# Grouped-query layer: transposes and a small product moved in front of two score tiles, behind the weighing

## The chip, the cores and the metric

One core of a Trainium2 chip runs the whole kernel as one program. The metric is the device time of one execution in microseconds (us); shown are the median and the spread of three runs. Engines are named as in the profile: PE is TensorE (its weight loads are PEld), DVE is VectorE, ACT is ScalarE, POOL is GpSimd, SP is SyncE.

## The reference

Four transformer-like layers run in a row over x of 8 batches x 512 tokens x 256 features in float32. Each layer normalises x and adds an attention-like part and a feed-forward part to it. The change is in the second layer (called layer 1 in the code), cut here to what matters:

```python
# attention: 16 query heads of width 16, 4 key/value heads, rotary positions
scores = einsum('bhqd,bhkd->bhqk', q, k) / sqrt(256)
p = softmax(scores, axis=-1)
o = einsum('bhqk,bhkd->bhqd', p, v);  attn = o.reshape(B, S, 256) @ Wo
# feed-forward: 64 slots, a gated update of them, and a read by the routing weights alpha
h = gelu(x @ w1x.T + b1);  alpha = softmax over the top 8 of (h @ w2.T + b2) / (|tau| + 0.1)
gi = (alpha.T @ x) / (sum of alpha over tokens)
S_new = GRU(gi, slots)                      # r, z = sigmoid, n = tanh
out = (alpha @ (S_new @ wv.T + bv)) @ wo.T + bo
```

## The kernel before

Layer 1 works batch by batch. Its loop is software-pipelined: one round of MAIN1 holds the back part of one batch (weighing the values, slot update, output) and the front part of the next (projections, scores for the row maxima). PRE1 is the front of the first batch alone, POST1 the back of the last alone, and MAIN1 is run 7 times between them. Each engine has its own instruction stream, written out by hand in program order (`pe1`, `dve1`, `act1`, `sp1`), and the streams meet only at semaphores.

The 16 heads are handled in 4 groups g of 4 heads. For each group the kernel makes two things from queries and keys:

- **Score tiles** `("S", g, i)`, i = 0 to 15, 128 queries x 512 keys. PE makes them in pairs (`two_scores`, L1455), and DVE takes the row maximum of each (`dve_max`, L910). After the 16th, `dve_split_max` (L916, L918) splits the maxima, PE transposes them (tile `("M", g)`, `pe_max_rows`, L543), ACT copies them to `mrow`, and SP sends them through DRAM into an extra row of the query tile.
- **Transposed scores** `("E", g, kt, hp)`, kt = 0 to 3 blocks of 128 keys, hp = 0, 1 pairs of heads (`pe_scores_t`, L557). ACT takes the exponential into `probs` (L816), and `pe_weigh` (L573) multiplies it with the values into `bank_u`.

When a group's four weighings are done, ACT copies `bank_u` to `uraw` (L803), PE transposes that with four transposes into tile `("DT", g)` (`pe_turn_sums`, L756), and DVE normalises it: `dve_normalise_heads` (reciprocal L924, multiply L926, then it waits for its own result and frees the tile). The slot update ends in `h_new` (DVE `blend_slots`, three operations, the last L1766); PE multiplies it with `wvs` into tile `"SV"` (4 products, 8 matmul records in the trace, L1565) and ACT moves it to `svT` (L1649).

**The ring.** The tiles S, M, DT, SV, L, GX, AT, SI and Z2 share three PSUM banks in strict rotation (`Ring` named `sc`: `bank0`, `bank1`, `bank_m`). The rotation follows the order in which `sc_plan1` lists the tiles. The tile at place n can be written only when the reader of the tile at place n-3 has freed it (`vacated`). The reader is DVE for S and DT, ACT for M and SV. `two_scores` waits for both banks of a pair before it issues either.

**Order on PE, groups 2 and 3.** While group 2 is weighed, the score tiles of the next batch's group 0 are made, and while group 3 is weighed those of group 1. For one kt the order is: E of hp 0, two scores (`maxima(0)`), E of hp 1, weighing of the block before (`pe_weigh`), two scores (`maxima(1)`). So a pair of scores stands behind each weighing, and the next pair follows with only one E between. The extra pieces stand behind the second pair:

- g = 2, kt = 1: scores 6 and 7, then DT of group 1.
- g = 2, kt = 3: scores 14 and 15, then (behind the kt loop) SV.
- g = 3, kt = 1: scores 6 and 7, then M of group 0, then DT of group 2.

DVE's stream has the same order: maxima 2 to 5 of group 0, `blend_slots`, maxima 6 and 7, normalise group 1, maxima 8 to 15 and their split, maxima 0 to 7 of group 1, normalise group 2, maxima 8 to 15.

Of the kernel before, what the change touches and what calls it, by code (L numbers as in the profile page):

```python
# [14 lines left out]
P = 128  # L15
BATCH, SEQ, DIM = 8, 512, 256
TT = SEQ // P
KT = DIM // P
# [33 lines left out]
def plans(plan0, plan1, plan2, plan3):  # L52

    return [plan0(FRONT[s], BACK[s]) for s in (PRE0, MAIN0, POST0)] + [plan1(FRONT[s], BACK[s]) for s in (PRE1, MAIN1, POST1)] + plan2 \
        + [plan3(FRONT[s], BACK[s]) for s in (PRE3, MAIN3, POST3)]
# [79 lines left out]
def s_uses(g):  # L135
    return [(("S", g, i), "dve") for i in range(GH * TT)]


def turn_uses(g):
    return [(("DT", g), "dve")]  # L140
# [5 lines left out]
def m_use(g):  # L146
    return [(("M", g), "act")]
# [15 lines left out]
def parts_of(front, back, *items):  # L163

    return [u for part, uses in items if (front if part == "front" else back) for u in uses]
# [24 lines left out]
def sc_plan1(front, back):  # L190
    return parts_of(front, back, ("back", [("AT", "act"), ("SI", "dve")] + s_uses(2)[8:10] + m_use(1) + s_uses(2)[10:]),
                    ("back", s_uses(3)[:8] + m_use(2) + s_uses(3)[8:12]), ("front", [("L", "dve")]),
                    ("back", turn_uses(0) + s_uses(3)[12:] + [("GX", "dve")]),
                    ("front", s_uses(0)[:2]), ("back", m_use(3)), ("front", s_uses(0)[2:8]), ("back", turn_uses(1)),
                    ("front", s_uses(0)[8:]), ("back", [("SV", "act")]),
                    ("front", s_uses(1)[:8] + m_use(0)), ("back", turn_uses(2)), ("front", s_uses(1)[8:]),
                    ("back", [("Z2", "act")]), ("front", s_uses(2)[:2]), ("back", turn_uses(3)), ("front", s_uses(2)[2:8]))


# [63 lines left out]
def build(nc, d, out):  # L263
    ctx = ExitStack()
    with ctx:
# [63 lines left out]
        sc = Ring(sem, "sc", banks + [bank_m], plans(sc_plan0, sc_plan1, NOTHING, sc_plan3))  # L329
# [207 lines left out]
        def pe_max_rows(pe, l, it, g):  # L537

            pe.wait_ge(*maxima_ready(l, it, g))
            for s in sc.vacated(l, it, ("M", g)):  # L540
                pe.wait_ge(*s)
            for qt in range(TT):
                ins = nc.tensor.transpose(sc.tile(l, ("M", g))[0:8, qt * P:(qt + 1) * P],  # L543
                                          msplit[:, g % 2, qt, :, :].rearrange("p a h -> p (a h)"), ident[:])
            ins.then_inc(sc.full.sem, 1)
# [203 lines left out]
        def pe_turn_sums(pe, l, it, g):  # L749

            for s in sc.vacated(l, it, ("DT", g)):
                pe.wait_ge(*s)
            fence(pe)
            pe.wait_ge(*done(pu, l, it, ("U", g)))
            for t in range(TT):
                ins = nc.tensor.transpose(sc.tile(l, ("DT", g))[:, t * P:(t + 1) * P], uraw[:, g % 2, t * P:(t + 1) * P],  # L756
                                          ident[:])
            ins.then_inc(sc.full.sem, 1)
# [514 lines left out]
        wvs = sb("wvs", [P, KT, DIM], F32, l1)  # L1273
# [39 lines left out]
        h_new = sb("h_new", [P, KT, 64], F32, l1)  # L1313
# [24 lines left out]
        h_done = sig("h_done", [0, 1, 0, 0], "vector")  # L1338
# [91 lines left out]
        def pe1(pe, l, it):  # L1430
            front, back = FRONT[l], BACK[l]
# [55 lines left out]
            if back:  # L1487
# [6 lines left out]
                for t in range(TT):  # L1494
                    ins = nc.tensor.transpose(sc.tile(l, "AT")[0:64, t * P:(t + 1) * P], alpha[:, t, :], ident[:])
# [3 lines left out]
                for f in range(KT + 1):  # L1499
                    for t in range(TT):  # L1500
                        lhs = xn[:, t, f * P:(f + 1) * P] if f < KT else ones_sq[:]
                        ins = nc.tensor.matmul(sc.tile(l, "SI")[:, f * 64:(f + 1) * 64], lhs, alpha[:, t, :],
                                               start=(t == 0), stop=(t == TT - 1))
                ins.then_inc(sc.full.sem, 1)
            for g in range(GROUPS):
                for kt in range(TT):
                    cut = SHARE1[2 * kt:2 * kt + 3] if g == 1 else [4 * kt, 4 * kt + 2, 4 * kt + 4]
                    if g == 0:
                        cut = [8 + 2 * kt, 10 + 2 * kt, 10 + 2 * kt]
                    if g == 1 and kt == 0 and not front:  # L1510
                        cut = [0] + cut[1:]

                    def maxima(j):
                        if back if g < 2 else front:
                            scores_of((g + 2) % GROUPS, cut[j], cut[j + 1])

                    if back:
                        pe_scores_t(pe, l, it, g, kt, pair, lambda: maxima(0))
                        if kt == 0 and g < GROUPS - 1:
                            pe_max_rows(pe, l, it, g + 1)  # L1520
                    else:
                        maxima(0)
                    if back and (g or kt):
                        pe_weigh(pe, l, it, GROUPS * g + kt - 1, kv_of_group)
                    if front and g == 0 and kt == 1:
                        pe_transpose_xn(pe, l, it)
                    maxima(1)
                    if front and g == 3 and kt == 1:
                        pe_max_rows(pe, l, it, 0)
                    if front and g == 1 and kt == 1:  # L1530
                        for s in sc.vacated(l, it, "L"):
                            pe.wait_ge(*s)
                        pe.wait_ge(*done(st, l, it, "H"))
                        for t in range(TT):
                            ins = nc.tensor.matmul(sc.tile(l, "L")[:, t * 64:(t + 1) * 64], hid1[:, t * P:(t + 1) * P], w21[:],
                                                   start=True, stop=True)
                        ins.then_inc(sc.full.sem, 1)
                    if back and g and kt == 1:
                        pe_turn_sums(pe, l, it, g - 1)
                if front and g == 0:  # L1540
                    pe.wait_ge(*done(st, l, it, "T"))
                    project("QQ", 0, wq1[:, :, 0:P])
                    last_maxima(0, 2)
                    project("QQ", 1, wq1[:, :, P:2 * P])
                    last_maxima(2, 4)
                    project("KK", 0, wk1[:, :, 0, :], 64)
                    project("KK", 1, wk1[:, :, 1, :], 64)
                    project("H", 0, w1x, P, 1)
                    last_maxima(4, 6)
                if back and g == 1:  # L1550
                    for s in sc.vacated(l, it, "GX"):
                        pe.wait_ge(*s)
                    pe.wait_ge(*gi_done.at(l, it, 1))
                    for j in range(6):
                        for k_ in range(KT):
                            ins = nc.tensor.matmul(sc.tile(l, "GX")[:, j * 64:(j + 1) * 64], wih[:, k_, j * P:(j + 1) * P],
                                                   gi[:, k_, :], start=(k_ == 0), stop=(k_ == 1))
                    ins.then_inc(sc.full.sem, 1)
                if back and g == 2:
                    for s in sc.vacated(l, it, "SV"):  # L1560
                        pe.wait_ge(*s)
                    pe.wait_ge(*h_done.at(l, it, 1))
                    for m in range(KT):
                        for k_ in range(KT):
                            ins = nc.tensor.matmul(sc.tile(l, "SV")[:, m * 64:(m + 1) * 64], wvs[:, k_, m * P:(m + 1) * P],  # L1565
                                                   h_new[:, k_, :], start=(k_ == 0), stop=(k_ == 1))
                    ins.then_inc(sc.full.sem, 1)
            if back:
                for s in sc.vacated(l, it, "Z2"):
# [2 lines left out]
                for k_ in range(KT):  # L1572
                    ins = nc.tensor.matmul(sc.tile(l, "Z2")[0:64, 0:DIM], svT[:, k_, :], wos[:, k_, :],
                                           start=(k_ == 0), stop=(k_ == 1))
# [8 lines left out]
            if back:  # L1583
# [3 lines left out]
                for t in range(TT):  # L1587
                    nc.tensor.matmul(st.tile(l, "OUT")[:, t * DIM:(t + 1) * DIM], alphaT[:, t * P:(t + 1) * P], sv2[:],
                                     start=(t % 2 == 0), stop=False)
# [69 lines left out]
        def dve1(dve, l, it, step):  # L1659
            front, back = FRONT[l], BACK[l]  # L1660
# [107 lines left out]
            def maxima(g, first, last):  # L1768
                for i in range(first, last):
                    dve_max(dve, l, it, step, g, i)  # L1770
                if last == 16:
                    dve_split_max(dve, l, it, step, g, ("S", g, 15))
# [45 lines left out]
            if back:  # L1818
                blend_slots()
            for g in range(2):  # L1820
                for first, last in ((0 if g else 6, 8), (8, 16)):
                    if front:
                        maxima(g, first, last)
                    if back and last == 8:
                        dve_normalise_heads(dve, l, it, step, g + 1)
            if front:
                maxima(2, 0, 2)
# [1677 lines left out]
```

## Time and profile before

| | us |
|---|---|
| median of 3 runs | 3073.55 |
| lowest, highest | 3070.24, 3075.05 |
| profiled execution, its own time | 3092.09 |
| profiled execution, span from first to last instruction | 3090.4 |

| engine | busy us | share of the span |
|---|---|---|
| PE | 2780.4 | 90% |
| DVE | 1868.2 | 60% |
| ACT | 1387.8 | 45% |
| POOL | 394.5 | 13% |

Busy times are sums over the whole span, in which four layers with different limits follow each other. A busy share therefore tells little of one stage: the stage is read from the order of instructions in it, and from what ended each wait. The profiled execution lies 18.5 us above the median of the timed runs; a difference worked out from it is added to the median. Clock is the granted clock of TensorE as a share of full speed (1.00 is 2.4 GHz).

### The profile page before, as it was taken

What the parts mean: (1) busy time and instruction counts of PE and PEld (TensorE: products, weight loads), DVE (VectorE), ACT (ScalarE), POOL (GpSimd) and SP (SyncE); (2) the same over time, 40 slices, a digit from 0 to 9 for tenths busy, and PEclk for the clock granted to TensorE, in tenths of its full rate; (3) what the DMA queues carried; (4) which work ended last, traced back from release to release, by engine and by line L of the source; (5) the groups of instructions that cost most, each with busy time, mean ns of one, the idle gap of its engine ahead of it and who ended that gap; (6) DMA issues with size and microseconds to landing.
All of it is one profiled execution on the core that took longest, in us unless ns stands there. A gap on an engine that the chain in (4) does not pass through costs nothing.

```text
span 3090.4 us, 53706 instructions
## 1 busy us (share of the span) xinstructions
PE 2780.4 (90%) x15686; PEld 1805.8 (58%) x15687; DVE 1868.2 (60%) x4512; ACT 1387.8 (45%) x2011; POOL 394.5 (13%) x373
## 2 busy tenths in 40 slices
PE   4999999999988888888879999999899579999998
PEld 2566556546644444443437777776666356666666
DVE  5666666666637777777737677772122456566653
ACT  1644554454433555555545455432233144444443
POOL 1011001100100000000021211221111312222220
PEclk7999999999987999999999999999999789999999
DMA  6534543654412122221214111122311233333330
GB/s 193 166 119 139 171 140 104 180 152 138 119 39 88 56 70 70 70 69 56 70 51 166 46 36 54 48 89 71 109 62 60 89 98 105 103 102 102 101 98 16
DMA packets 157951, 294.55 MB, mean 95 GB/s; under 512 B 24928, under 2 KB 82657, under 8 KB 149057
## 3 DMA queue, kind: packets, MB, share of 16 engines
q1 hardware_dynamic: 145264, 259.59, 27.8%
q0 software_dynamic: 10464, 28.59, 3.0%
q10 hardware_dynamic: 2160, 5.61, 0.5%
q8 instruction: 31, 0.51, 0.1%
q14 instruction: 32, 0.25, 0.0%
HBM read 194.02 MB, written 99.68 MB: 95 GB/s over the span
## 4 chain that ended last, share of the span: by engine, by line
PE 69%; DVE 12%; DMA 6%; issue 6%; ACT 4%; SPq 2%; DVEq 0%; another core or an unknown queue 0%; POOL 0%; ACTq 0%; POOLq 0%
PE bank_u L573 6%; PE pair L557 5%; PE pair L616 4%; PE bank L1984 4%; PE pair L733 4%; PE pair L2134 4%; DVE nmax L910 3%; PE pair L3074 3%; PE pair L777 3%; PE bank_m L3038 3%; PE bank L534 3%; PE bank L3038 3%; PE bank L2589 3%; PE pair L1482 2%; DMA k_a<-parts_dram 2%
## 5 line engine op out<-in xcount | busy, mean ns | idle before, releaser
L816 ACT ACTIVATE probs<-pair 128x1024 f32<-128x1024 f32 x512 | 502.1, 1021 | 218.7 <-PE pair L557 217.9
L910 DVE TENSOR_REDUCE nmax<-bank 128x1 f32<-128x512 f32 x664 | 441.8, 685 | 175.1 <-PE bank L534 127.0
L910 DVE TENSOR_REDUCE nmax<-bank_m 128x1 f32<-128x512 f32 x360 | 246.5, 685 | 106.7 <-PE bank_m L534 59.8
L573 PE MATMUL bank_u<-probs,vext 128*32 128x512 f32 x2048 | 288.7, 637 | 0.6 <-ACT uraw L803 0.5
L557 PE MATMUL pair<-q_a,k_a 98*128 98x512 f32 x512 | 176.4, 450 | 22.2 <-ACT probs L816 11.8
L534 PE MATMUL bank<-k_a,q_a 96*128 96x512 f32 x336 | 149.3, 479 | 27.4 <-DMA k_a<-parts_dram 24.0
L2282 DVE CUSTOM_DVE_ANT_0 bank<-bank,mask_q 128x128 f32<-128x128 f32 (+1 forms) x320 | 118.8, 420 | 89.5 <-PE bank_m L2024 67.1
L557 PEld LDWEIGHTS pair<-q_a,k_a 98*128 98x128 f32 x512 | 90.3, 202 | 122.0 <-ACT probs L816 66.4
L797 ACT ACTIVATE mrow<-bank 8x512 f32<-8x512 f32 x87 | 50.2, 577 | 231.1 <-PE bank L543 231.1
L2134 PE MATMUL pair<-fc,hid 128*128 128x256 f32 x512 | 133.2, 399 | 6.3 <-ACT probs L2175 6.3
L1455 PE MATMUL bank<-k,q 62*128 62x512 f32 x302 | 113.2, 478 | 26.7 <-DVE nmax L910 26.7
L3110 DVE TENSOR_TENSOR mid<-bank,gate 128x352 f32<-128x352 f32 x73 | 38.3, 524 | 162.1 <-PE bank L3038 162.0
L733 PE MATMUL pair<-w2e,hid 128*128 128x256 f32 x512 | 131.0, 381 | 3.3 <-ACT probs L816 3.3
L557 PE MATMUL pair<-q,k 64*128 64x512 f32 x512 | 116.7, 454 | 15.8 <-DMA q<-m_dram 7.8
L2175 ACT ACTIVATE probs<-pair 128x1024 f32<-128x1024 f32 (+1 forms) x128 | 112.2, 917 | 36.0 <-PE pair L2053 34.5
L474 POOL TENSOR_SCALAR veps<-mv 128x4 f32<-128x4 f32 x31 | 7.3, 235 | 843.9 <-DVE mv L468 839.6
L2967 POOL DMA_INDIRECT xg<-xn,posi x64 | 62.8, 982 | 401.4 <-DVE posi L2815 316.4
L733 PEld LDWEIGHTS pair<-w2e,hid 128*128 128x128 f32 x512 | 94.7, 190 | 30.5 <-issue 15.6
L2134 PEld LDWEIGHTS pair<-fc,hid 128*128 128x128 f32 x512 | 93.1, 194 | 25.5 <-ACT probs L2175 8.2
L534 PEld LDWEIGHTS bank<-k_a,q_a 96*128 96x128 f32 x336 | 65.6, 197 | 72.2 <-DVE nmax L910 26.5
L3074 PE MATMUL pair<-moe_c,midT 128*128 (+1 forms) x432 | 107.2, 384 | 0.0
L803 ACT ACTIVATE uraw<-bank_u 128x512 f32<-128x512 f32 x96 | 57.1, 594 | 110.7 <-PE bank_u L2065 58.9
(471 smaller groups left out, 6036.9 us busy)
## 6 DMA issues: line engine op xcount, KB each, us to landing
parts_dram<-parts SPq DMA_DIRECT2D x64, 512.0 KB
q<-parts_dram SPq DMA_DIRECT2D x126, 128.0 KB
q_a<-parts_dram SPq DMA_DIRECT2D x31, 512.0 KB
k_a<-parts_dram SPq DMA_DIRECT2D x31, 512.0 KB
xs<-xres SPq DMA_DIRECT2D x24, 512.0 KB, 3.1
xl<-xs SPq DMA_DIRECT2D x24, 512.0 KB, 3.9
x_in<-xg SPq DMA_DIRECT2D x74, 128.0 KB, 2.1
yg_dram<-y_out POOLq DMA_DIRECT2D x72, 128.0 KB, 2.0
```

The lines of the kernel that those rows point to most:

```text
L534: nc.tensor.matmul(sc.tile(l, name)[:], q(g, h)[:, qt * P:(qt + 1) * P].bitcast(F32R), k(g, h).bitcast(F32R), start=True, stop=True).then_ ...
L557: ins = nc.tensor.matmul(st.tile(l, name)[:, hh * SEQ:(hh + 1) * SEQ], k[:, kt * P:(kt + 1) * P].bitcast(F32R), q.bitcast(F32R), start=Tru ...
L573: ins = nc.tensor.matmul(bank_u[32 * h:32 * h + 32, :], vext[:, kt, kv(g, h), :], probs[:, kt % 2, h * SEQ:(h + 1) * SEQ], start=(kt == 0) ...
L616: ins = nc.tensor.matmul(st.tile(l, name)[:, half * SEQ:(half + 1) * SEQ], weight[:, k_, m * P:(m + 1) * P].bitcast(F32R), turned[:, k_, : ...
L733: nc.tensor.matmul(st.tile(l, "OUT")[:, t * DIM:(t + 1) * DIM], hid0[:, i, t * P:(t + 1) * P], w2e[:, i, :], start=(i == 0 and t % 2 == 0) ...
L816: nc.scalar.activation(probs[:, kt % 2, hp * 2 * SEQ:hp * 2 * SEQ + n], st.tile(l, name)[:, 0:n], ACT.Exp).then_inc(st.free["act"].sem, 1)
L910: nc.vector.tensor_reduce(nmax[:, g % 2, qt, h:h + 1], sc.tile(l, name)[:], AX, ALU.max, negate=True).then_inc(sc.free["dve"].sem, 1)
L1984: ins = nc.tensor.matmul(dst, lefts[i](k).bitcast(F32R), rights[j](k).bitcast(F32R), start=(first and n == 0 and k == 0), stop=(last and n ...
L2134: nc.tensor.matmul(st.tile(l, "OUT")[:, t * DIM:(t + 1) * DIM], hid3[:, i, t * P:(t + 1) * P], fc2[:, i, :], start=(i == 0 and t % 2 == 0) ...
L2282: ins = nc.vector.tensor_tensor_reduce(here, here, mask_q[:, at:DIM], -1.0, LARGEST, ALU.add, ALU.min, nmax[:, g % 2, qt, h:h + 1])
L3038: ins = nc.tensor.matmul(s2.tile(l, name)[:, 0:352], x_inT[:, n, k * P:(k + 1) * P], moe_ab[:, bass.ds(e, 1), k, 352 * j:352 * j + 352].re ...
L3074: ins = nc.tensor.matmul(st.tile(l, ("Y", n))[:, 0:DIM], midT[0:w, n, i * P:(i + 1) * P], moe_c[0:w, bass.ds(e[n], 1), i, :].rearrange("p ...
```

## The change

The three extra pieces in groups 2 and 3 move to directly behind the weighing, ahead of the pair of scores that stood there. DT of group 2 and M of group 0 also change places with each other. `sc_plan1` lists the tiles in the new order, so the rotation of the banks changes with it, and DVE normalises group 1 ahead of maximum 6 of group 0, and group 2 ahead of maximum 6 of group 1. The streams of ACT, POOL and SP are not edited. No instruction is added or removed. The lines left out in the diff behind `h_done` are the loop with `wvs` that stands in the removed block.

```diff
 def sc_plan1(front, back):
-                    ("front", s_uses(0)[:2]), ("back", m_use(3)), ("front", s_uses(0)[2:8]), ("back", turn_uses(1)),
-                    ("front", s_uses(0)[8:]), ("back", [("SV", "act")]),
-                    ("front", s_uses(1)[:8] + m_use(0)), ("back", turn_uses(2)), ("front", s_uses(1)[8:]),
+                    ("front", s_uses(0)[:2]), ("back", m_use(3)), ("front", s_uses(0)[2:6]), ("back", turn_uses(1)),
+                    ("front", s_uses(0)[6:14]), ("back", [("SV", "act")]), ("front", s_uses(0)[14:]),
+                    ("front", s_uses(1)[:6]), ("back", turn_uses(2)), ("front", m_use(0) + s_uses(1)[6:]),
...
 def pe1(pe, l, it):
                         pe_weigh(pe, l, it, GROUPS * g + kt - 1, kv_of_group)
                     if front and g == 0 and kt == 1:
                         pe_transpose_xn(pe, l, it)
-                    maxima(1)
+                    if back and g > 1 and kt == 1:
+                        pe_turn_sums(pe, l, it, g - 1)
                     if front and g == 3 and kt == 1:
                         pe_max_rows(pe, l, it, 0)
+                    if back and g == 2 and kt == TT - 1:
+                        for s in sc.vacated(l, it, "SV"):
+                            pe.wait_ge(*s)
+                        pe.wait_ge(*h_done.at(l, it, 1))
...
+                        ins.then_inc(sc.full.sem, 1)
+                    maxima(1)
...
-                    if back and g and kt == 1:
+                    if back and g == 1 and kt == 1:
                         pe_turn_sums(pe, l, it, g - 1)
...
-                if back and g == 2:
-                    for s in sc.vacated(l, it, "SV"):
-                        pe.wait_ge(*s)
-                    pe.wait_ge(*h_done.at(l, it, 1))
-                    for m in range(KT):
-                        for k_ in range(KT):
-                            ins = nc.tensor.matmul(sc.tile(l, "SV")[:, m * 64:(m + 1) * 64], wvs[:, k_, m * P:(m + 1) * P],
-                                                   h_new[:, k_, :], start=(k_ == 0), stop=(k_ == 1))
-                    ins.then_inc(sc.full.sem, 1)
...
 def dve1(dve, l, it, step):
             for g in range(2):
-                for first, last in ((0 if g else 6, 8), (8, 16)):
+                for first, last in ((0 if g else 6, 6), (6, 16)):
                     if front:
                         maxima(g, first, last)
-                    if back and last == 8:
+                    if back and last == 6:
                         dve_normalise_heads(dve, l, it, step, g + 1)
```

## Rows read from the trace of the kernel before

**Rows 1.** The page: busy us, share of the span, instructions of each engine.

```profile
PE 2780.4 (90%) x15686; PEld 1805.8 (58%) x15687; DVE 1868.2 (60%) x4512; ACT 1387.8 (45%) x2011; POOL 394.5 (13%) x373
```

**Rows 2.** Busy times by stretch: two rounds (start:end us, length, busy us of each engine, clock).

```profile
1042.20:1123.65 81.45, 71.40 (x438) 34.89 (x437) 63.22 (x137) 45.96 (x63) 3.63 (x3) 1.00 0.22 66
1368.00:1449.40 81.40, 72.82 (x406) 37.94 (x408) 58.89 (x130) 42.09 (x59) 3.63 (x3) 0.92 0.21 65
```

**Rows 3.** Waits in MAIN1, 1042.2 to 1530.8 us: waiter, releaser, total, times, longest.

```profile
PE bank L1455 <- DVE nmax L910: 20.3, 35, 0.9
PE bank_m L1455 <- DVE nmax L910: 13.1, 17, 1.1
```

**Rows 4.** The line of SV: instructions, first and last start.

```profile
L1565 PE MATMUL bank<-h_new,wvs x56: 275/275/323, 1028.9 to 1523.3; 128*128 128x64 f32 x56
```

**Rows 5.** PE in order of time around DT of group 1 (start, us, [idle before]).

```profile
1101.36 0.50 PE L1455 MATMUL bank<-k,q 62*128 62x512 f32 x2 [0.91 <-DVE nmax L910]
1101.70 0.40 PE L557 MATMUL pair<-q,k 64*128 64x512 f32 x2
1102.03 1.07 PE L573 MATMUL bank_u<-probs,vext 128*32 128x512 f32 x8
...
1103.46 0.66 PE L756 MATMUL bank<-ident,uraw 128*128 128x128 f32 x4
...
1105.30 0.49 PE L1455 MATMUL bank_m<-k,q 62*128 62x512 f32 x1 [0.75 <-DVE nmax L910]
```

**Rows 6.** DVE in order of time there.

```profile
1103.75 0.29 DVE L1766 TENSOR_TENSOR h_new<-gru 128x128 f32<-128x128 f32 x1
1103.96 0.68 DVE L910 TENSOR_REDUCE nmax<-bank_m 128x1 f32<-128x512 f32 x1
1104.56 0.68 DVE L910 TENSOR_REDUCE nmax<-bank 128x1 f32<-128x512 f32 x1
1105.16 0.24 DVE L924 RECIPROCAL rt<-bank 128x16 f32<-128x16 f32 x1
...
1106.09 0.69 DVE L910 TENSOR_REDUCE nmax<-bank_m 128x1 f32<-128x512 f32 x1 [0.22 <-DVE heads L926]
```

**Rows 7.** PE around SV and behind it.

```profile
1108.25 0.50 PE L1455 MATMUL bank<-k,q 62*128 62x512 f32 x2 [0.55 <-DVE nmax L910]
...
1108.92 1.06 PE L573 MATMUL bank_u<-probs,vext 128*32 128x512 f32 x8
1109.92 0.50 PE L1455 MATMUL bank_m<-k,q 62*128 62x512 f32 x1
...
1110.35 1.10 PE L1565 MATMUL bank<-h_new,wvs 128*128 128x64 f32 x8
1111.38 0.50 PE L557 MATMUL pair<-q,k 64*128 64x512 f32 x2
1111.80 0.50 PE L1455 MATMUL bank_m<-k,q 62*128 62x512 f32 x1
```

**Rows 8.** DVE in order of time: maximum 14 of group 0, end of the split.

```profile
1110.46 0.69 DVE L910 TENSOR_REDUCE nmax<-bank_m 128x1 f32<-128x512 f32 x1 [0.37 <-PE bank L1455]
...
1111.99 0.17 DVE L918 TENSOR_TENSOR msplit<-nmax,msplit 128x16 fp32r<-128x16 f32 x1
```

**Rows 9.** All engines around M of group 0 and DT of group 2.

```profile
1116.85 0.60 PE L543 MATMUL bank<-ident,msplit 128*8 128x128 f32 x4
...
1117.57 0.59 ACT L797 ACTIVATE mrow<-bank 8x512 f32<-8x512 f32 x1 [1.01 <-PE bank L543]
...
1117.80 0.63 PE L756 MATMUL bank_m<-ident,uraw 128*128 128x128 f32 x4 [0.35 <-DVE nmax L910]
1118.36 0.50 PE L557 MATMUL pair<-q,k 64*128 64x512 f32 x2
...
1118.46 0.26 DVE L924 RECIPROCAL rt<-bank_m 128x16 f32<-128x16 f32 x1 [0.21 <-PE bank_m L756]
...
1119.26 1.07 PE L573 MATMUL bank_u<-probs,vext 128*32 128x512 f32 x8
```

More of the change, by code:

```diff
@@ L1526, in pe1 @@
                         pe_transpose_xn(pe, l, it)
-                    maxima(1)
+                    if back and g > 1 and kt == 1:
+                        pe_turn_sums(pe, l, it, g - 1)
                     if front and g == 3 and kt == 1:
                         pe_max_rows(pe, l, it, 0)
+                    if back and g == 2 and kt == TT - 1:
+                        for s in sc.vacated(l, it, "SV"):
+                            pe.wait_ge(*s)
+                        pe.wait_ge(*h_done.at(l, it, 1))
+                        for m in range(KT):
+                            for k_ in range(KT):
+                                ins = nc.tensor.matmul(sc.tile(l, "SV")[:, m * 64:(m + 1) * 64], wvs[:, k_, m * P:(m + 1) * P],
+                                                       h_new[:, k_, :], start=(k_ == 0), stop=(k_ == 1))
+                        ins.then_inc(sc.full.sem, 1)
+                    maxima(1)
                     if front and g == 1 and kt == 1:
```

## The prediction

> **What bounds the kernel now.** I read the page first. PE is busy for 2780.4 us, 90% of the span, and DVE for 60% [rows 1]; over the whole kernel nothing but PE can be the bound. That is an average over four layers, so the second view is the busy times cut into rounds of MAIN1. The reader is to see in it that a round takes 81.4 us, that PE works for 71.4 of them and DVE for 63.2, at a clock of 1.00 [rows 2]. PE leads, but about 10 us of a round are gaps. The third view, the waits of this stage, tells what closes some of them: PE's score products, in front of a bank whose maximum DVE has not taken, 20.3 and 13.1 us in total over 52 waits, none over 1.1 us [rows 3]. So the stage is neither PE's nor DVE's alone; it is a relay of two engines through three banks. What a moved piece is worth depends on whether it stands in a gap or in front of one. That is read from the fourth view, the order of time, with one round followed from 1101 to 1120 us.
>
> **The law of the relay.** Two kinds of distance alternate between pairs of scores. Behind a weighing, the next pair comes 1.00 us after the weighing's start: 1108.92 to 1109.92 [rows 7]. That is long enough for DVE, and no wait stands there. Where only one E lies between two pairs, PE would be ready 0.34 us (pair) and 0.33 us (E) later (1101.36, 1101.70, 1102.03) [rows 5]. But the second tile of the next pair needs the bank of the first tile of this pair (three banks, places n and n-3). DVE starts on that tile 0.54 us after the pair's start (1109.92 to 1110.46) [rows 7, 8], takes 0.69 us, and PE follows 0.06 us behind its end (1104.56 + 0.68 = 1105.24, then 1105.30) [rows 5, 6]. Sum 1.29 us: two pairs with one E between them are at least 1.29 us apart, and PE idles for about 0.55 us, as at 1108.25 [rows 7]. **Before, the extra pieces stand in exactly that distance, and fill the wait. After, they stand behind the weighing, where no wait was.** Each piece then costs its own time and the 0.55 us wait opens beside it, unless the old place held a wait for another reason. So I work out each of the three places.
>
> **Place 1, DT of group 1.** Before: scores 6 and 7 at 1103.03 (0.43 ahead of DT, the distance of a pair to a transposition or small product: 1109.92 to 1110.35), DT at 1103.46, and scores 8 and 9 only at 1105.30, 0.75 us of it idle [rows 5, 7]. DVE is late there: it ends `blend_slots` and starts on maximum 6 at 1103.96, takes 7 at 1104.56 and frees it at 1105.24 [rows 6]. After: DT starts at 1103.03 (its bank, of score 3, and ACT's copy of the sums, which the weighing waits for as well, are both ready). Four transposes take 0.56 us on PE (1117.80 to 1118.36) [rows 9], so scores 6 and 7 start at 1103.59. DVE is ready for the reciprocal at 1103.96 as before; the normalising takes 0.93 us up to the next maximum (1105.16 to 1106.09) [rows 6]. Maximum 6 thus starts at 1104.89, ends at 1105.58, and scores 8 and 9 (9 needs the bank of 6, 8 that of DT) start at 1105.64. **Later by 0.34 us.** Before, DVE had to take two maxima ahead of this release; now it has a normalising and one maximum, 0.93 instead of 0.60. Behind it all distances are the old ones: scores 12 and 13 move from 1108.25 to 1108.59.
>
> **Place 2, SV.** Before: scores 14 and 15 at 1109.92, SV at 1110.35, E at 1111.38 (SV takes 1.03), scores 0 and 1 of the next group at 1111.80, with 0.09 us of wait: SV hides DVE's two maxima [rows 7]. After: the weighing starts at 1109.26, SV at 1110.26 (`h_new` was written at 1103.75 + 0.29 [rows 6], so that wait is over), scores 14 and 15 at 1111.29. Score 1 needs the bank of 14, hence 1111.29 + 1.29 = 1112.58. Score 0 needs ACT to have left SV. ACT starts on M 0.72 us after M, which takes 0.60, and copies it in 0.59 us [rows 9]; with SV's 1.03 that makes about 1.15 and 0.6 us, done by 1112.0 by this estimate, so it is covered; were ACT late by 0.6 us more, it would set the pair. **Later by 1112.58 - 1111.80 = 0.78, of which 0.44 is new.** The split of the maxima, which ends 1.70 us after maximum 14 begins (1110.46 to 1111.99 + 0.17) [rows 8], ends at 1111.83 + 1.70 = 1113.53 and holds up maximum 0; its release at 1114.28 meets a pair that is ready at 1114.25. That is nothing.
>
> **Place 3, DT of group 2 and M of group 0.** Before: weighing over at 1116.42, scores 6 and 7, M at 1116.85, 0.35 us of wait for maximum 6, DT at 1117.80, E at 1118.36, scores 8 and 9 right behind it without a wait, weighing at 1119.26 [rows 9]: 2.84 us in all. After, from the weighing's end at T: DT at T, M at T + 0.56, ready for the pair at T + 1.16. But score 7 takes the bank of DT. DVE starts the reciprocal 0.66 us after DT (1117.80 to 1118.46) [rows 9], needs 0.93, plus 0.06: the pair goes at T + 1.65, a wait of half a microsecond that did not exist. Then only an E lies between it and scores 8 and 9, so they go 1.29 later, at T + 2.94; pair and E follow, and the weighing starts at T + 3.61. **0.77 us are new.** Score 8 takes the bank of M; ACT starts on that 0.72 us after M (1116.85 to 1117.57) and takes 0.59, so it has left it at T + 1.9, a microsecond ahead of need. Queued behind the waiting pair are E of kt 2, hence ACT's exponentials, and everything PE does later in the round. On SP, the store and load of the maxima go out about 0.9 us later, hidden, for the next round uses them only behind the rest of group 3 and the whole output. The stack loads that wait for an E move with PE, and nothing at the old times waited for them.
>
> **The sum.** 0.34 + 0.44 + 0.77 = 1.55 us a round. Nothing gives it back within the round: what bounds PE from there to the output are waits for DVE and ACT that themselves follow PE. SV has 56 matmul records in MAIN1 [rows 4], 8 a round, so 7 rounds: 10.9 us. In POST1 no scores of a next batch exist, and the moved pieces have the same neighbours as before: 0. In PRE1 M stands two scores earlier in a stream that DVE bounds: 0, half a microsecond either way. On the profiled execution's own time that is 3092.09 + 10.9 = 3103.0; the median of the runs lies 18.5 us lower, and the rounds that I counted stand at full clock, so I add the same 10.9 us to it: **3084.4 us**.
>
> Bounds of the terms: place 1 between 0 (the normalising fits into DVE's time during `blend_slots`) and 0.6 (the pair waits for maximum 7 too); place 2 between 0.1 (SV's old place hid only part) and 0.8 (ACT sets it); place 3 between 0.4 (one of the two waits) and 1.0. Sums 0.5 to 2.4 a round, 3.5 to 17 us.
>
> **Rivals.** 0.2% of this kernel is 6.1 us, about what a measurement can tell from no change.
> (a) *Faster: the wait at the old places goes and none comes.* The two waits of 0.75 and 0.35 us that end behind DT and M today [rows 5, 9] vanish: 7 x 1.10 = 7.7 us, 3065.9. It decides at place 1 by whether DVE can take maximum 6 when it lands, at 1103.59 + 0.54 = 1104.13. It could only if DVE were free; it is in `blend_slots` until 1103.96 and has 0.93 us of normalising ahead. Against it also: the distance with one E alone shows 0.55 us of wait every time. Chance 0.09.
> (b) *Within 0.2%: only the third place costs, or the loss is taken up by a later wait.* 7 x 0.77 = 5.4 us, 3079.0. For it: about 10 us of gaps a round. Against it: these gaps end with work of DVE or ACT that started behind PE's. Chance 0.15.
> (c) *The clock falls more often.* A round of MAIN1 shows 0.92 in place of 1.00 [rows 2]. From the first to the last record of SV there are 494.4 us, six rounds and SV's own 0.8 or so: 82.3 a round, against 81.4 at full clock, so about 5 us went to that one fall [rows 2, 4]. If the new waits brought one in each of the six other rounds, it would be 10.9 + 30 = 41 us, 3114. For it: the new waits cut PE's share a little, 71.4 of 83.0 us for 71.4 of 81.4. Against it: waits of 0.55 and 1.1 us stand in every round at clock 1.00. The Trainium skill (TensorE: Matmul & The Clock Gate, "A second HAM failure mode: psum-queue depth-cycling") tells of a kernel whose clock swung because PE idled briefly between groups of matmuls that cycle through PSUM banks. By that rule the change would bring (c); the trace does not agree so far, since these rounds cycle in that way and keep the full clock but for one. Chance 0.03.
>
> **Chances and range.** The forecast, all three places costing, has 0.73. Faster 0.09, within 0.2% 0.15, slower 0.76 (the forecast and (c)). The range goes from 3076 to 3091: the bounds 3.5 and 17 us, with its foot inside (b). It leaves out (a), (c) and a part of (b).
>
> **What the profile after should show.** A round from SV to SV 1.55 us longer at full clock. DT of group 1 directly behind a weighing; scores 8 and 9 behind it still with a wait for DVE, some 0.9 us. SV, then a pair, E, and a wait of about 0.6 us in front of scores 0 and 1 where there was 0.09. DT and M back to back, then a wait of about 0.5 us for DVE's normalising in front of scores 6 and 7, and one of about 0.6 in front of 8 and 9. PE's busy time unchanged. The prediction is wrong if the pair behind DT and M goes without a wait, if scores 0 and 1 follow their E directly, or if the round's other waits shrink by what these add.

## The result, and the profile after

The kernel after takes 3102.59 us (median of 6 runs, 3100.58 to 3113.18) against 3074.3 us (6 runs) before: a ratio of 1.009, 95% interval 1.0074 to 1.0106. It is 28 us slower, where 10.9 us was forecast. The direction was right. The time lies outside the stated range of 3076 to 3091 us.

The first view to read is the busy time of the rounds of MAIN1, cut here at the first product with `svT` (L1575 in the new line numbers). Columns as in [rows 2]: start:end, length, busy us of PE, PEld, DVE, ACT and POOL, granted clock, DMA.

```profile
1040.47:1128.36 87.89, 77.05 (x439) 39.12 (x437) 63.26 (x137) 46.44 (x63) 3.63 (x3) 0.92 0.20 61
1128.36:1214.60 86.24, 75.39 (x439) 38.07 (x437) 63.28 (x137) 46.47 (x63) 3.62 (x3) 0.94 0.20 62
...
1476.60:1562.83 86.23, 75.38 (x438) 38.11 (x436) 63.27 (x137) 46.47 (x63) 3.63 (x3) 0.94 0.20 62
```

A round takes 86.2 or 87.9 us in turn, not 83.0. The column that gives it away is the clock: 0.92 or 0.94 in each of the six rounds, where five of six stood at 1.00 before. (The second stretch of [rows 2] is not a whole round: it has 406 PE instructions for 438. The round with the low clock, cut at the products with `svT`, takes 86.50 us.)

```profile
1367.88:1454.38 86.50, 77.37 (x439) 39.36 (x437) 63.25 (x137) 46.08 (x63) 3.63 (x3) 0.92 0.20 62
```

PE is "busier" than before, 75.4 us for 71.4 [rows 2], with the same instructions. The six rounds together take 522.36 us against 493.55 before, 28.8 us more. (The profiled executions differ by only 12 us: the one of before is 16 us longer behind the last SV and 3 us longer ahead of the first, and 2 us shorter from the last SV but one to the last; its own time was 18.5 us above the median.)

The second view is PE in order of time in the second round, at the three places. Place 1, DT of group 1, answers to [rows 5]:

```profile
1105.33 1.06 PE L573 MATMUL bank_u<-probs,vext 128*32 128x512 f32 x8
1106.33 0.66 PE L756 MATMUL bank_m<-ident,uraw 128*128 128x128 f32 x4
1106.91 0.50 PE L1455 MATMUL bank<-k,q 62*128 62x512 f32 x2
1107.25 0.40 PE L557 MATMUL pair<-q,k 64*128 64x512 f32 x2
1108.94 0.49 PE L1455 MATMUL bank_m<-k,q 62*128 62x512 f32 x1 [1.29 <-DVE nmax L910]
```

From the weighing to scores 8 and 9 it is 3.61 us, against 3.27 before (1102.03 to 1105.30): 0.34 more, as worked out. Place 2, SV, answers to [rows 7]:

```profile
1111.89 0.50 PE L1455 MATMUL bank<-k,q 62*128 62x512 f32 x2 [0.55 <-DVE nmax L910]
...
1113.56 1.10 PE L1537 MATMUL bank_m<-h_new,wvs 128*128 128x64 f32 x8
1114.59 0.50 PE L1455 MATMUL bank<-k,q 62*128 62x512 f32 x2
...
1115.88 0.50 PE L1455 MATMUL bank_m<-k,q 62*128 62x512 f32 x1 [0.55 <-DVE nmax L910]
```

From scores 12 and 13 to the first pair of the next group it is 3.99 us against 3.55: 0.44, and the wait of 0.55 us has opened that SV used to hide. Place 3 answers to [rows 9]; all engines:

```profile
1120.50 0.66 PE L756 MATMUL bank_m<-ident,uraw 128*128 128x128 f32 x4
...
1120.99 0.60 PE L543 MATMUL bank<-ident,msplit 128*8 128x128 f32 x4
1121.19 0.26 DVE L924 RECIPROCAL rt<-bank_m 128x16 f32<-128x16 f32 x1 [0.53 <-PE bank_m L756]
...
1122.02 0.50 PE L1455 MATMUL bank<-k,q 62*128 62x512 f32 x1 [0.43 <-DVEq L930]
...
1123.31 0.50 PE L1455 MATMUL bank<-k,q 62*128 62x512 f32 x2 [0.55 <-DVE nmax L910]
```

The wait in front of scores 6 and 7 is for line 930, DVE's release behind the normalising. From the end of the weighing at 1120.50 to the next weighing at 1123.98 there are 3.48 us, forecast 3.61, before 2.84: 0.64 more. So the three places cost 0.34 + 0.44 + 0.64 = 1.42 us a round. That is not what makes a round 4.8 or 6.5 us longer. The rest is further on, behind the output, in the same timeline of PE (1136 to 1150 us):

```profile
1136.84 3.72 PE L777 MATMUL pair<-wo,oc 128*128 128x256 f32 x16 [0.68 <-ACT oc L807]
1141.99 2.00 PE L513 MATMUL pair<-wv,xnT 128*128 128x64 f32 x16 [1.43 <-DVE xres L937]
1143.83 0.84 PE L1495 MATMUL bank<-ident,alpha 128*64 128x128 f32 x4
1144.47 3.51 PE L1502 MATMUL bank<-alpha,xn 128*128 128x64 f32 x16
1147.77 1.91 PE L1502 MATMUL bank<-alpha,ones_sq 128*128 128x64 f32 x8
```

and in the kernel before, the same wait and the same two groups, at full clock:

```profile
1055.85 2.00 PE L513 MATMUL pair<-wv,xnT 128*128 128x64 f32 x16 [1.43 <-DVE xres L937]
...
1058.12 1.90 PE L1502 MATMUL bank<-alpha,xn 128*128 128x64 f32 x16
1059.85 1.06 PE L1502 MATMUL bank<-alpha,ones_sq 128*128 128x64 f32 x8
```

The same 24 products take 5.42 us in place of 2.96, nearly twice as long. The clock by stretch, in the same round of the kernel after, shows why:

```profile
1128.36:1143.00 14.64, 11.80 (x67) 8.04 (x66) 11.03 (x23) 2.00 (x3) 0.00 (x0) 1.00 0.23 72
1143.00:1145.00 2.00, 2.00 (x17) 1.96 (x16) 1.25 (x9) 0.29 (x1) 0.94 (x2) 0.76 0.76 262
1145.00:1155.00 10.00, 10.00 (x47) 6.74 (x47) 4.85 (x11) 4.63 (x6) 1.32 (x2) 0.54 0.16 54
1155.00:1163.00 8.00, 7.55 (x47) 3.15 (x44) 3.00 (x7) 4.79 (x5) 1.36 (x1) 1.00 0.01 2
```

One to two microseconds after PE's wait of 1.43 us for DVE's addition, TensorE drops to half clock (1.2 GHz) for 10 to 14 us. I call this a fall. It stands in each of the six rounds of the kernel after, 14.7 to 15.7 us behind the first product with `svT`, and in one of six rounds before, though the wait of 1.43 us stands in every round of both. The first round of the kernel after and the one round of the kernel before have a second, shorter fall as well, 49 us behind that product. None of the instructions around it was touched by the change.

### The profile page after: what moved, and what is told of

It is laid out like the page before. It is cut to its first block, busy times and chain, and to the rows that moved or that the text cites. A ratio compares the mean times of both kernels' runs of the same rounds, so it can differ in the third digit from the quotient of the medians.

```text
span 3102.5 us, 53706 instructions
## 1 busy us (share of the span) xinstructions
PE 2797.3 (90%) x15686; PEld 1822.4 (59%) x15687; DVE 1872.6 (60%) x4512; ACT 1390.8 (45%) x2011; POOL 393.9 (13%) x373
## 4 chain that ended last, share of the span: by engine, by line
PE 68%; DVE 12%; issue 6%; DMA 6%; ACT 4%; POOL 2%; SPq 2%; DVEq 0%; ACTq 0%; POOLq 0%
PE bank_u L573 6%; PE pair L557 5%; PE pair L616 4%; PE bank L1986 4%; PE pair L733 4%; PE pair L2136 3%; DVE nmax L910 3%; PE bank L2591 3%; PE bank_m L3040 3%; PE pair L777 3%; PE pair L3076 3%; PE bank L534 3%; PE bank L3040 3%; PE pair L1482 2%; DMA k_a<-parts_dram 2%
## 5 line engine op out<-in xcount | busy, mean ns | idle before, releaser
L910 DVE TENSOR_REDUCE nmax<-bank 128x1 f32<-128x512 f32 x679 | 451.5, 686 | 195.5 <-PE bank L534 125.8
L910 DVE TENSOR_REDUCE nmax<-bank_m 128x1 f32<-128x512 f32 x345 | 236.5, 685 | 93.9 <-PE bank_m L534 62.8
L557 PEld LDWEIGHTS pair<-q_a,k_a 98*128 98x128 f32 x512 | 87.8, 197 | 117.5 <-ACT probs L816 65.7
L1455 PEld LDWEIGHTS bank<-k,q 62*128 62x128 f32 x316 | 46.2, 192 | 100.7 <-DVE nmax L910 87.6
```

Source lines behind the costliest of these rows:

```text
L557: ins = nc.tensor.matmul(st.tile(l, name)[:, hh * SEQ:(hh + 1) * SEQ], k[:, kt * P:(kt + 1) * P].bitcast(F32R), q.bitcast(F32R), start=Tru ...
L910: nc.vector.tensor_reduce(nmax[:, g % 2, qt, h:h + 1], sc.tile(l, name)[:], AX, ALU.max, negate=True).then_inc(sc.free["dve"].sem, 1)
L1455: ins = nc.tensor.matmul(sc.tile(l, ("S", g, i + j))[:], q(g, h)[:, qt * P:(qt + 1) * P].bitcast(F32R), k(g, h).bitcast(F32R), start=True, ...
```

## The experiments

Two theories share the result. **A, the relay**: the moved pieces stand where no wait was, and the waits that they used to fill open; 1.42 us a round. **B, the clock**: in a longer round the output's wait is followed by a fall, which costs 3 to 5 us. The rival to B, called C in the first expectations, is that the moved pieces bring the falls themselves. All figures are medians; the ratio is to the kernel before, run on the same chip. The length of a round is that at full clock, where the profile has such a round. Counts of falls are of the one profiled execution of each kernel.

**One place at a time.** Each of the three kernels makes one of the moves, with its part of `sc_plan1` and of DVE's order. The first, for instance:

```diff
+                    if back and g == 2 and kt == 1:
+                        pe_turn_sums(pe, l, it, g - 1)
                     maxima(1)
...
-                    if back and g and kt == 1:
+                    if back and g in (1, 3) and kt == 1:
                         pe_turn_sums(pe, l, it, g - 1)
```

> Only the transposes of group 1 are moved. Theory A (relay): the local shift is 0.34 us a round, 2.4 us over the 7 rounds, at full clock a round of 81.75 us. Theory B (the clock): each round also has a stretch at half clock behind the output in which PE loses about 5 us, as the kernel after has; whether it comes depends on where the wait of 1.43 us in front of the values falls, and so on the length of the round. A alone gives +2.4 us on the kernel before; A with a fall in every round +30 us; B leaves open which of the two a length of 81.75 us gives. Rival C (each moved piece brings its own fall): +10 us for this third.

> Only the slots' products are moved. Theory A: 0.44 us a round in front of the first pair of group 1, 3.1 us in all, a round of 81.85 us at full clock. Theory B: the same and, if the clock falls in every round, about 5 us more a round, 35 us in all. Rival C: about 10 us for this third.

> Only the transposes of group 2 and of the maxima of group 0 are moved. Theory A: 0.77 us a round, 5.4 us in all, a round of 82.2 us at full clock. Theory B: the same and up to 5 us a round more if the clock falls in every round. Rival C: about 10 us for this third.

DT of group 1 alone: 3078.31 us, 1.0024 (1.0012 to 1.0036). Its rounds:

```profile
1127.78:1212.94 85.16, 75.51 (x439) 38.04 (x437) 63.33 (x137) 46.08 (x63) 3.63 (x3) 0.94 0.21 63
1212.94:1294.66 81.72, 71.15 (x438) 34.81 (x437) 63.31 (x137) 45.95 (x63) 3.63 (x3) 1.00 0.22 66
```

SV alone: 3078.77 us, 1.0014 (0.9999 to 1.003):

```profile
1295.71:1380.94 85.23, 75.52 (x439) 37.98 (x437) 63.15 (x137) 46.39 (x63) 3.63 (x3) 0.94 0.21 63
1380.94:1462.76 81.82, 71.22 (x438) 34.81 (x436) 63.13 (x137) 46.26 (x63) 3.63 (x3) 1.00 0.22 66
```

DT of group 2 with M alone: 3095.61 us, 1.0078 (1.0057 to 1.01):

```profile
1039.16:1127.51 88.35, 78.61 (x439) 39.82 (x437) 63.31 (x137) 46.23 (x63) 3.64 (x3) 0.90 0.20 61
1127.51:1212.96 85.45, 75.67 (x439) 38.16 (x437) 63.23 (x137) 46.19 (x63) 3.63 (x3) 0.94 0.22 63
```

SV's interval reaches just below 1, so its loss is not clear of noise by time; the length of its rounds is. The full-clock rounds give theory A its terms: 81.75 and 81.82 us are 0.34 and 0.42 above 81.40. One fall costs 3.4 us (85.16 less 81.72, 85.23 less 81.82), so the third kernel's 85.45, which has no full-clock round, is read as 82.05 with a fall, 0.65 more. Sum 1.41. Counted in the first six rounds, the fall behind the output comes in 2, 4 and 6 of them. That it comes in runs (in the first two rounds, the first four, all) speaks for something that repeats with the round. C forecast 10 us for each, and gets 4, 5 and 22: it falls for the first two. But the third piece could still be special.

**The same round, made longer by neutral work.** These kernels are the kernel before, in its old order, with one pair of E products (group 3, kt 2, heads 2 and 3) computed several times into the same tile. Each repeat costs 0.24 us.

```diff
-                for hh in range(2):
+                for hh in list(range(2)) * (1 + again * hp):
...
-                        pe_scores_t(pe, l, it, g, kt, pair, lambda: maxima(0))
+                        pe_scores_t(pe, l, it, g, kt, pair, lambda: maxima(0), 4 if l == MAIN1 and g == 3 and kt == 2 else 0)
```

> The kernel before with one pair of E products of group 3 (kt 2, second pair of heads) computed five times instead of once, into the same tile: no tile order and no wait is changed, only the round is longer, by 4 x about 0.24 us. Theory B (a round's length decides whether the half-clock stretch behind the output comes): rounds of 82.4 us at full clock and, with a fall in most rounds, of 85.5 to 86; 7 x 1.0 = 7 us by the work alone, up to 30 us with the falls. Rival (the change's own waits bring the falls): 7 us and no more falls than before, 3081 us.

> The same with seven times instead of once: the round longer by about 1.45 us, which is nearly what the change adds (1.56). Theory B: about the time of the kernel after, rounds of 86 to 88 us, 3098 to 3103 us. Rival: 10 us from the work alone, 3084 us, with rounds of 82.9 us at clock 1.00.

With four repeats 3109.8 us, 1.0122 (1.0102 to 1.0143); with six 3107.69 us, 1.0114 (1.0093 to 1.0136). Rounds of the first, then of the second kernel:

```profile
1306.26:1394.90 88.64, 79.50 (x447) 40.76 (x445) 63.31 (x137) 46.20 (x63) 3.64 (x3) 0.90 0.20 61
1483.51:1569.25 85.74, 76.61 (x447) 39.13 (x445) 63.24 (x137) 46.15 (x63) 3.63 (x3) 0.94 0.20 63
```

```profile
1045.03:1132.80 87.77, 78.65 (x451) 40.31 (x449) 63.26 (x137) 46.19 (x63) 3.62 (x3) 0.92 0.20 61
1132.80:1219.00 86.20, 77.06 (x451) 39.35 (x449) 63.27 (x137) 46.19 (x63) 3.62 (x3) 0.94 0.20 62
```

These kernels have none of the change in them and take no less time than it. The second, whose rounds are lengthened as much as by the change, shows the very rhythm of the kernel after in its first four rounds, 87.8 and 86.2 us in turn. So many falls need none of the moved pieces. With four repeats 6.5 us of work costs 36 us. Five of its six rounds have two falls, the one behind the output and a shorter one, 49 us behind the `svT` product: 88.64 us is the 82.33 of a full-clock round (seen in a later kernel) plus 3.4 and 2.9. Both kernels ran over what B had forecast.

**More work, less time.** The kernel after, with the same pair computed three times.

```diff
-                        pe_scores_t(pe, l, it, g, kt, pair, lambda: maxima(0))
+                        pe_scores_t(pe, l, it, g, kt, pair, lambda: maxima(0), 2 if l == MAIN1 and g == 3 and kt == 2 else 0)
```

> The kernel after with that pair computed three times instead of once, which adds about 0.5 us of work to each round. Theory B: the length 83.0 us is one at which every round meets a fall, and another length need not be; with falls in a part of the rounds only, the time would be 3090 to 3098 us, less than the kernel after though it does more work. Rival (the falls are set by what the round holds, not by its length): 3.5 us more than the kernel after, 3106 us.

3092.17 us, 1.0068 (1.0046 to 1.0089): 10 us less than the kernel after, with 3.3 us more to do. The two were not run side by side, and the intervals of their ratios overlap; but no run of the one (3089.84 to 3097.0) reaches the lowest of the other (3100.58), and the six traced rounds take 511 us for 522. Its rounds:

```profile
1122.26:1205.56 83.30, 71.55 (x442) 35.10 (x441) 63.26 (x137) 46.35 (x63) 3.62 (x3) 1.00 0.22 65
1205.56:1295.18 89.62, 78.77 (x443) 40.46 (x441) 63.32 (x137) 46.54 (x63) 3.63 (x3) 0.90 0.20 60
1295.18:1378.48 83.30, 71.56 (x442) 35.09 (x440) 63.26 (x137) 46.37 (x63) 3.63 (x3) 1.00 0.21 65
```

Four of six rounds are at full clock now. A longer round is not always a worse one. Falls behind the output in the six rounds (second falls not counted), by the full-clock length of a round:

| round, us | kernel | falls |
|---|---|---|
| 81.40 | before | 1 |
| 81.75 | DT of group 1 moved | 2 |
| 81.82 | SV moved | 4 |
| 82.05 | DT of group 2 and M moved | 6 |
| 82.33 | before, four repeats | 6 |
| 82.83 | after | 6 |
| 82.84 | before, six repeats | 5 |
| 83.30 | after, two repeats | 2 |

The profiles of four of these kernels have no round at full clock. Their lengths are worked out (82.05 as above, 82.84 as 81.40 plus six repeats of 0.24) or taken from later kernels that add work only inside waits (82.33, 82.83; 85.74 and 86.23 with one fall, less 3.4, give the same). Each count is of one execution, and the length may not fix it: the profiled execution of SV, with four falls, was the slowest of ten (3086.32 us, mean clock 0.954); the fastest took 3070.72 us at 0.959. The difference is about what four falls of 3.4 us cost, though only the one was traced. The table shows a tendency with length, 1 to 6 and back to 2, and no law.

**Work in the wait.** The fall follows PE's wait of 1.43 us. These kernels let PE work through it: products of the identity with a weight, into `bank_u`, whose content nobody needs at that moment and which the next weighing overwrites.

```diff
                 pe_out_heads(pe, l, it, wo1)
+            if l == MAIN1:
+                for n in range(3):
+                    nc.tensor.matmul(bank_u[:, 0:DIM], ident[:], wo1[:, 0, :], start=True, stop=True)
```

> The kernel after, with three products more in each round of MAIN1 (identity by a weight, 128x256, into bank_u, read by nobody) behind the output's products, where PE waits 1.43 us for DVE's addition. Theory B: the half-clock stretch follows this wait, and goes when PE works through it: every round at clock 1.00 and 82.97 us long, 3084 us in all, 18 us less than the kernel after. Rival (the falls are set by something else, say by the waits that the change brings): rounds of 86 to 88 us stay, 3102 us or a little more.

> The kernel before with the three products that nobody reads behind the output's products, as in the after_fill run. Theory B: what falls stand behind the output go; there was one in seven rounds of the profile, so 0 to 5 us less, 3069 to 3074 us. Rival (the added products delay the values, or only move the falls to the next wait of PE, 45 us later): 3074 to 3080 us.

> The kernel after with one product that nobody reads behind the output's products instead of three, 0.39 of the 1.43 us of wait filled. The length of the round is that of the after_fill run. Theory B (the wait of PE there is what the half-clock stretch follows): about one microsecond of wait is left, so the falls 14 to 16 us behind the last slots' product should stay in all or most rounds, 3095 to 3103 us. Rival (any added product changes it by shifting things): 3087 us as with three.

> The slowest kernel so far (round longer by 0.95 us of repeated work, a fall in every round, 3110 us) with the three products in the wait. Theory B: the falls behind the output go, what stays is 7 x 0.95 = 6.7 us of work and at most short falls 45 us later: 3077 to 3086 us. Rival (a round of this length is slow whatever PE does in the wait): 3105 us or more.

Kernel after with three products: 3087.03 us, 1.0039 (1.0019 to 1.0059), 15 us less. The falls behind the output are gone, and a full-clock round shows. I had expected all rounds at full clock and 3084 us. Shorter falls stand in five of six rounds, 45 to 46 us behind the `svT` product, behind waits of about 1.1 and 0.55 us for DVE at the start of group 1. The kernel after had one such fall; four have come with the filling. They cost 1.55 or 2.9 us each, 10 us in six rounds, for the 25 that went:

```profile
1171.14 0.49 PE L1455 MATMUL bank_m<-k,q 62*128 62x512 f32 x1 [1.09 <-DVE nmax L910]
```

```profile
1127.35:1213.10 85.75, 75.28 (x445) 37.34 (x443) 63.37 (x137) 46.37 (x63) 3.62 (x3) 0.96 0.20 63
1383.22:1466.05 82.83, 72.37 (x444) 35.85 (x442) 63.25 (x137) 46.33 (x63) 3.62 (x3) 1.00 0.21 65
```

Kernel before with three: 3069.82 us, 0.999 (0.998 to 1.0), no more than just measurable; in its profile only one short fall is left. With one product instead of three, the kernel after takes 3094.28 us, 1.0068 (1.0045 to 1.0091): two of six rounds had the fall behind the output. I had expected it in most of them, so a third of the filling did about half of the work, in one profile and four runs. The kernel with four repeats and three products takes 3092.22 us, 1.0061 (1.0042 to 1.0081), 18 us less than without them. I had expected 3077 to 3086: all falls behind the output are gone, 3.4 us a round, but in five of six rounds the second fall is still there, 45 to 46 us behind the `svT` product, at 2.9 us each. It was in five of six rounds of the unfilled kernel too, which my expectation left out:

```profile
1124.14:1209.38 85.24, 76.49 (x453) 38.26 (x451) 63.36 (x137) 46.11 (x63) 3.63 (x3) 0.96 0.21 63
1209.38:1291.71 82.33, 73.59 (x453) 36.78 (x451) 63.23 (x137) 46.06 (x63) 3.63 (x3) 1.00 0.21 65
```

**Both waits, and a version that beats both kernels.** Besides the three products, the pair of E products of group 1 (kt 0, heads 2 and 3) is computed four times, 0.72 us of work ahead of the second place:

```diff
-                        pe_scores_t(pe, l, it, g, kt, pair, lambda: maxima(0))
+                        pe_scores_t(pe, l, it, g, kt, pair, lambda: maxima(0), 3 if l == MAIN1 and g == 1 and kt == 0 else 0)
```

> The kernel before with the three products in the output's wait, and one pair of E products of group 1 (kt 0, second pair of heads) computed four times: 0.72 us of work ahead of a wait of 1.08 us for DVE in which it should be hidden, 44 us behind the last slots' product, where the other falls stand. Theory B: rounds of 81.4 us at clock 1.00 throughout, 3066 to 3070 us. Rival (the added work is not hidden): 3 to 5 us more than with the three products alone, 3073 to 3075 us.

> The kernel after with the same work in both waits that kept the kernel before at full clock in every round. What is left between the two is the relay alone. Theory A with B: rounds of 82.83 us at clock 1.00, which is 1.42 us more than 81.41, so 10 us more than the kernel before with both waits worked through (3067.3 us): 3077 us, with no or few falls. Rival (the moved pieces bring falls of their own at their three places): 3085 us or more.

On the kernel before this gives 3067.34 us, 0.9979 (0.9969 to 0.9989), the lowest time of this study; its interval overlaps that of the three products alone. PE in order of time at the second place and behind the output, and one of its rounds:

```profile
1078.93 0.50 PE L1455 MATMUL bank_m<-k,q 62*128 62x512 f32 x1 [0.39 <-DVE nmax L910]
...
1128.61 1.46 PE L1600 MATMUL bank_u<-wo,ident 128*128 128x256 f32 x6
1130.20 2.00 PE L513 MATMUL pair<-wv,xnT 128*128 128x64 f32 x16
```

```profile
1279.40:1360.80 81.40, 73.34 (x450) 36.53 (x448) 63.23 (x137) 45.95 (x63) 3.62 (x3) 1.00 0.22 66
```

The output's wait is gone from the record, the one at the second place is down from 1.1 to 0.39 us, the values start no later (26.92 us behind SV here and in the kernel before), and the round keeps its 81.4 us: both pieces of added work lie inside waits. All six rounds stand at clock 1.00. On the kernel after, the same gives 3076.14 us, 1.0002 (0.999 to 1.0014), again with each of the six rounds at 1.00, where C had 3085 us or more:

```profile
1119.38:1202.20 82.82, 73.05 (x450) 36.34 (x448) 63.24 (x137) 46.38 (x63) 3.63 (x3) 1.00 0.21 65
```

So with the moved pieces in place and both waits worked through, no fall comes: C is out. It also shows that a round of 82.83 us does not bring falls by its length alone; the waits have to be there. 82.82 less 81.40 is 1.42 us: the relay by itself. Over seven rounds that is 9.9 us, and the two kernels lie 8.8 us apart (not run side by side; their ratios to the kernel before, 1.0002 and 0.9979, make it 7).

## Why the prediction was right about the places and wrong about the time

- **The law of the relay** held to a few hundredths. Pairs with one E between them are 1.29 us apart in the kernel after too (1122.02 to 1123.31). Place 1 came out at 0.34 (forecast 0.34), place 2 at 0.44 (0.44), each also when moved alone (0.34, 0.42).
- **Place 3** was sized at 0.77 and measured 0.64. The bank of DT was free 0.83 us after the reciprocal began (1121.19 to 1122.02), where I had taken the 0.93 up to DVE's next maximum plus 0.06 for the release: the release comes ahead of DVE's next start. The sum, 1.42 for 1.55, makes 9.9 us for 10.9. None of the signs named as proof against the prediction came. Two of its details were off: the wait in front of scores 8 and 9 is 1.29 us, not some 0.9, and PE's busy time did not stay, since products at half clock take longer.
- **"The rounds that I counted stand at full clock, so I add the same 10.9 us"** is the step that failed. Five of six stood at full clock in the kernel before, and in the kernel after none did. The runs put in its place: six rounds of the kernel after take 522.4 us, of which 6 x 82.83 = 497.0 at full clock, so 25.4 went to falls, against 5.1 before (493.55 less 6 x 81.41). 20.3 us of falls and 8.5 of relay make the 28.8.
- **Rival (c)** named the effect, more falls, with 0.03 for a chance and 5 us for each round (measured 3.4 or 5.0); its cause, the new waits, was not the one. The evidence against it, that waits of 0.55 and 1.1 us stand in every round at full clock, was true, but the falls behind the output follow an old wait, of 1.43 us, that the change does not touch. The one stretch at 0.92 [rows 2] was the warning. The trace has a fall right behind that wait there (from 1382.8 us, 1.3 us after the wait ends), so such a fall was possible in every round, and nothing in the profile said what kept it away in the other five. The Trainium skill (TensorE: Matmul & The Clock Gate, "A second HAM failure mode: psum-queue depth-cycling") tells of a clock that swings because PE idles briefly between groups of matmuls. The runs agree in part: each fall behind the output comes behind an idle stretch of PE, 1.43 us, and goes when PE works there, and falls cost 25 us in six rounds. But the waits of 0.55 us that come from cycling through the banks stand in rounds at clock 1.00 as well, in the last kernel above in all six.
- **Rival (a)** fell as argued: DVE was in `blend_slots` when the pair landed, and the wait behind DT of group 1 grew from 0.75 to 1.29 us. **Rival (b)** fell too: no later wait shrank by what the places added.

Open: what decides whether the output's wait is followed by a fall. Shown is that rounds of other lengths gave other counts in the profiled executions, with or without the moved pieces, that the falls often come in runs of rounds, and that work in the wait removes them. The times and clocks of SV's ten runs speak for counts that also change from one execution of a kernel to the next. That a round with a fall, 3.4 us longer, puts the next one in the same position again is my reading of the runs (two rounds of 85.13 and 85.16 us, then none; four of 85.23 to 85.27, then none), and was not tried by itself.

## What to carry to other kernels

In a relay through few banks, put extra PE work between the two pairs that wait for each other, not behind a long piece that already covers the reader. Where a loop shows even one round with a lower clock, find the wait ahead of it before you add up microseconds: a change elsewhere in the round can then cost or give several times its own size, as the repeats did here. To see the change by itself, compare both kernels with PE kept at work in those waits. Cheap products that nobody reads did that, and on the kernel before they gained 0.2% by themselves. Look at every wait, not only the longest: with one filled, falls came behind the next.

## What the runs showed of the hardware

- TensorE went from clock 1.00 to half clock one to two microseconds after the end of a wait of 1.43 us, with small products behind it. A fall of 10 us cost the round 3.4 us, most of it in products of 64 columns (3.51 us for 16 that take 1.90 otherwise); one of 14 us cost 5.0. The same wait also stood in rounds at clock 1.00, five of six in the kernel before.
- 3.3 us more of work in the rounds took 10 us off the kernel after (3102.6 to 3092.2), and 6.5 us more put 36 us on the kernel before (3073.5 to 3109.8).
- Adding 1.46 us of products into a wait of 1.43 us removed every fall behind it in the traced rounds of five kernels and did not lengthen a round at full clock (81.4 us in the kernel before, with them and without).
